# Second attention of a four-layer model rewritten with queries on partitions, and semaphores zeroed one phase later

## The reference, cut to what matters

```
L1:  xn = x * rsqrt(mean(x*x) + 1e-6) * norm1_w;  scale, shift = cond @ film1_w + film1_b
     h  = xn * (1 + scale) + shift
     q, k, v = h @ q_w + q_b, h @ k_w + k_b, h @ v_w + v_b
     p  = softmax(q @ k.T / 16)                   # one head, 256 queries x 256 keys
     x  = x + (p @ v) @ proj_w + proj_b
```

## Time and profile before

| | |
|---|---|
| median of 3 runs | 3744.56 us (3743.07 to 3746.08) |
| profiled execution: time, span | 3743.7 us, 3741.9 us |
| L1a, first transfer to last write of x | 1103.85 to 1404.89 us: 301.04 us |
| busy share of the span: PE, DVE, ACT, POOL | 86%, 61%, 46%, 22% |
| mean granted clock of PE | 0.929 |

### The profile page before, as it was taken

One profiled execution on the slowest core, in us unless ns is written; L12 is line 12 of the kernel. 1 busy time (PEld: TensorE's weight loads), 2 busy tenths in 40 slices (PEclk: granted clock), 3 DMA queues, 4 the chain that ended last, 5 costly groups with the idle time before them and its releaser, 6 DMA issues. The chain is left out here.

```text
span 3741.9 us, 71958 instructions
## 1 busy us (share of the span) xinstructions
PE 3219.6 (86%) x26636; PEld 2628.5 (70%) x26636; DVE 2298.1 (61%) x4257; ACT 1712.5 (46%) x3102; POOL 809.2 (22%) x644
## 2 busy tenths in 40 slices
PE   5899999997988877979999699699999999971686
PEld 3677777775977767967777588477777776761576
DVE  3556665655656655657777566566656656637664
ACT  1344444443543324545455354466666666610353
POOL 1211111111111101112232211312212222130453
PEclk8999999998999888989999799799999999965798
DMA  4000000001010000010000000100000000030243
GB/s 146 10 6 6 6 3 6 6 6 32 23 31 0 0 0 24 0 64 0 0 0 0 30 17 23 49 1 0 0 0 0 0 0 0 0 115 2 77 117 66
DMA packets 64848, 80.79 MB, mean 22 GB/s; under 512 B 9730, under 2 KB 56706, under 8 KB 64500
## 3 DMA queue, kind: packets, MB, share of 16 engines
q1 hardware_dynamic: 58628, 71.27, 6.4%
q0 software_dynamic: 6144, 8.52, 1.2%
HBM read 66.93 MB, written 12.85 MB: 21 GB/s over the span
## 5 line engine op out<-in xcount | busy, mean ns | idle before, releaser
L1385 POOL TENSOR_TENSOR L0a_prob<-L0a_prob 128x1024 f32<-128x1024 f32 x48 | 117.1, 2439 | 570.9 <-PE L0a_o L1743 570.9
L1487 ACT ACTIVATE L0a_prob<-L0a_st 128x512 f32<-128x512 f32 x256 | 138.7, 596 | 201.1 <-PE L0a_st L1710 174.4
L1391 POOL TENSOR_TENSOR L3a_shift<-L3a_neg,L3a_mx 128x256 fp32r<-128x256 f32 x128 | 95.8, 749 | 555.9 <-DVE L3a_mx L1968 553.9
L1487 ACT ACTIVATE L3a_prob<-L3a_st 128x512 f32<-128x512 f32 x256 | 138.7, 596 | 128.5 <-PE L3a_st L1710 128.5
L1968 DVE TENSOR_REDUCE L0a_mx<-L0a_s 128x2 f32<-128x512 f32 x256 | 164.4, 684 | 39.3 <-PE L0a_s L1686 37.5
L2286 ACT ACTIVATE L2a_prob<-L2a_st 128x512 f32<-128x512 f32 x256 | 132.2, 603 | 117.6 <-PE L2a_st L2326 117.6
L1958 DVE SCALAR_TENSOR_TENSOR L3a_qk_lo<-L3a_raw,cols_sb,L3a_qk_hi 128x256 fp32r<-128x256 f32 x256 | 156.5, 651 | 36.6 <-ACT L3a_qk_hi L1478 36.6
L1968 DVE TENSOR_REDUCE L3a_mx<-L3a_s 128x2 f32<-128x512 f32 x256 | 163.8, 680 | 18.1 <-PE L3a_s L1686 18.1
L2563 DVE TENSOR_REDUCE L2a_mx<-L2a_s 128x2 fp32r<-128x512 f32 x256 | 163.5, 681 | 15.2 <-PE L2a_s L2326 15.2
L1907 DVE RECIPROCAL L0a_rsum<-L0a_sum 128x256 f32<-128x256 f32 x16 | 28.1, 1758 | 197.7 <-PE L0a_sum L1758 176.1
L1907 DVE RECIPROCAL L3a_rsum<-L3a_sum 128x256 f32<-128x256 f32 x16 | 28.1, 1758 | 174.4 <-PE L3a_sum L1758 155.3
(11 more groups left out here) (633 smaller groups left out, 11846.6 us busy)
## 6 DMA issues: line engine op xcount, KB each, us to landing
moe_stage<-in_moe_w SPq DMA_DIRECT2D x16, 1024.0 KB, 9.0
x_sb<-in_x SPq DMA_DIRECT2D x1, 4096.0 KB, 24.6
L0a_gate<-gate_rows SPq DMA_DIRECT2D x32, 128.0 KB, 3.8
L0m_gate<-gate_rows SPq DMA_DIRECT2D x32, 128.0 KB, 3.8
L2a_gates<-gate_rows SPq DMA_DIRECT2D x2, 2048.0 KB, 12.5
L2m_gate<-gate_rows SPq DMA_DIRECT2D x32, 128.0 KB, 3.8
out_x<-x_sb SPq DMA_DIRECT2D x1, 4096.0 KB, 14.2
token_rows<-x_sb SPq DMA_DIRECT2D x1, 4096.0 KB, 27.7
```

The source lines that it names most:

```text
L1385: nc.gpsimd.tensor_tensor(both[:, :, :, 0:N], both[:, :, :, 0:N], both[:, :, :, N:2 * N], ALU.add).then_inc(halves_done, 1)
L1391: nc.gpsimd.tensor_tensor(shift[:, u % 4, :, :, :], neg64[:].unsqueeze(1).unsqueeze(1).to_broadcast([P, 2, TT, 64]), mx[:, u % 2, :, :].un ...
L1487: A(prob[:, u % 4, h, :], st_ps[u % 2][h][:], ACT.Exp, scale=64 ** -0.5).then_inc(p_done, 1)
```

## The change

`attention` is removed, and `head256` written for the one-head case takes its place in `L1a`. The scores are made once, with queries on partitions and in three passes. DVE finds each row's maximum and scales it (`maxima`), ACT takes the exponential with that as its bias and gives the row's sum as a second output (`accum_out`), PE turns the exponentials with four 128x128 transposes (`turn_probs`), and ACT copies them to SBUF. The value product has no rows of sums. Instead the reciprocal of the two sums for each partition scales the projected output, in the instruction that adds it to x (`residual`). The bias of v is added from a row. POOL now normalises the tokens (line 398) besides adding the bias row. A pass of the loop holds the attention of batch i, q, k and v of batch i+1, the transposes and the modulation of i+2, the moments of i+3 and the projection of i-1. All four weight matrices have a buffer each and are loaded at once. SP zeroes, inside each phase and behind the transfers that it issues, the semaphores of the phase before; the block of POOL is gone. The last phase's are zeroed by SP in a block of their own.

```diff
-        yield sem
-        with nc.Block() as block:
-            @block.gpsimd
-            def _(pool):
-                for s in made:
-                    pool.sem_clear(s)
+    yield sem
+    g["used_ctx"].close()
+    g["used"], g["used_ctx"] = made, ctx
+
+def clear_used(engine, g):
+    for s in g["used"]:
+        engine.sem_clear(s)
...
-                  ("L1a", lambda: attention(nc, t, g, Attention("L1a", 1, 256, 256 ** -0.5, False, "rms", 1e-6))),
+                  ("L1a", lambda: head256(nc, t, g, "L1a")),
...
+        @block.sync                                  # head256
+            for n, name in enumerate(names):
+                sp.dma_start(raw[:, n, :]..., t[f"{nm}_{name}"]...).then_inc(w_in[n], 16)
+            sp.dma_start(y_row[:], t["L1_cond_proj_b"].partition_broadcast(P)).then_inc(rows_in, 16)
+            sp.wait_ge(rows_in, 16)
+            clear_used(sp, g)
+        @block.gpsimd
+            def tokens(j, first):
+                gated_wait(ve_done, j + 1)
+                nc.gpsimd.tensor_tensor(rstd[:], ve[:], g["mhalf"][:, 0:TT], ALU.pow).then_inc(rstd_done, 1)
+                if not first:
+                    gated_wait(tp_done, j)
+                nc.gpsimd.tensor_tensor(xn[:], tiles, rstd[:]..., ALU.mult).then_inc(xn_done, 1)
+                nc.gpsimd.tensor_tensor(tiles, tiles, y_row[:]..., ALU.add).then_inc(x_biased, 1)
+        @block.scalar
+            def x_hi(j, first):
+                act.wait_ge(xm_done, j + 1)
+                act.wait_ge(v_done, j)
+            def exponentials(j):
+                for qt in range(TT):
+                    act.wait_ge(nmx_done, TT * j + qt + 1)
+                    A(prob[:, qt, :], s_ps[qt][:, 0:N], ACT.Exp, bias=nmx[:, qt:qt + 1], scale=scale,
+                      accum_out=total[:, qt:qt + 1]).then_inc(p_done, 1)
+            def body(i, more, more2):
+                exponentials(i)
+                qk_hi(i + 1, 0)
+                act.wait_ge(pt_done, i + 1)
+                A(prob_t[:]..., pt_ps[:], ACT.Copy).then_inc(pt_taken, 1)
+                qk_hi(i + 1, 1)
+                x_hi(i + 2, False)
+                act.wait_ge(pv_done, i + 1)
+                A(o[0][:]..., o_ps[:], ACT.Copy).then_inc(ohi_done, 1)
+        @block.tensor
+            def scores(j, first):
+                pe.wait_ge(qklo_done, KD * j + KD)
+                pe.wait_ge(p_done, TT * j)
+                for qt in range(TT):
+                    for c in range(KD):
+                        last = three(s_ps[qt][:, 0:N], [x[:, c, qt * P:(qt + 1) * P] for x in q],
+                                     [x[:, c, :] for x in k_], c == 0, c == KD - 1)
+                    last.then_inc(s_done, 1)
+            def body(i, n, more, more2):
+                scores(i, n == 0)
+                queries_keys(i + 1, 0, False)
+                project(i - 1, n == 1, i + 2 if more else B)
+                turn_probs(i, n == 0)
+                queries_keys(i + 1, 1, False)
+                transposes(i + 2, n + 2)
+                values(i + 1, False)
+                weighted(i, n == 0)
+        @block.vector
+            def maxima(j):
+                for qt in range(TT):
+                    dve.wait_ge(s_done, TT * j + qt + 1)
+                    V.tensor_reduce(mx[:, qt:qt + 1], s_ps[qt][:, 0:N], AX.X, ALU.max).then_inc(mx_done, 1)
+                    dve.wait_ge(mx_done, TT * j + qt + 1)
+                    V.tensor_scalar(nmx[:, qt:qt + 1], mx[:, qt:qt + 1], -scale, None, ALU.mult).then_inc(nmx_done, 1)
+            def residual(j):
+                for tt in range(TT):
+                    V.scalar_tensor_tensor(x, y_ps[:, tt * D:(tt + 1) * D], share[:, tt:tt + 1], x, ALU.mult, ALU.add)
+            def body(i, first, more, more2, more3):
+                maxima(i)
+                take_values(i, first)
+                qk_low(i + 1, 0)
+                residual(i - 1)
+                shares(i, first)
+                moments(i + 3, False)
+                qk_low(i + 1, 1)
+                modulate(i + 2, False)
+                x_low(i + 2)
+                o_low(i)
```

More of the change, by code:

```diff
@@ L701, in _ @@
-            x_hi(0)
-            loader(act=act)[1]()
-            if masked:
-                act.wait_ge(kb_done, 1)
-            body(0, True, False)
-            with act.Fori(1, B - 1) as i:
-                body(i, False, False)
-            body(B - 1, False, True)
-            tail_rows(B - 1)
-            for n in range(a.pieces):
-                over(B - 1, n)
+            A = nc.scalar.activation
+            def x_hi(j, first):
+                act.wait_ge(xm_done, j + 1)
+                if not first:
+                    act.wait_ge(v_done, j)
+                A(xt[0][:], xm[:], ACT.Copy).then_inc(xhi_done, 1)
@@ L713, in _ @@
+            x_hi(0, True)
+            for n in range(4):
+                act.wait_ge(w_in[n], 16)
+                A(w_hi[:, n, :], raw[:, n, :], ACT.Copy).then_inc(whi_done, 1)
+            qk_hi(0, 0)
+            qk_hi(0, 1)
+            x_hi(1, False)
+            with act.Fori(0, B - 2) as i:
+                body(i, True, True)
+            body(B - 2, True, False)
+            body(B - 1, False, False)
         @block.tensor
@@ new lines, in weighted @@
+            def weighted(j, first):
+                pe.wait_ge(v_taken, j + 1)
+                pe.wait_ge(pt_taken, j + 1)
+                if not first:
+                    pe.wait_ge(olo_done, j)
+                for c in range(KD):
+                    for kt in range(TT):
+                        last = mm(o_ps[:, c * N:(c + 1) * N], v[:, kt, c * P:(c + 1) * P], prob_t[:, kt, :],
+                                  start=(kt == 0), stop=(kt == TT - 1))
+                last.then_inc(pv_done, 1)
@@ L943, in _ @@
+            body(B - 1, 2, False, False)
+            project(B - 1, False, B)
         @block.vector
@@ new lines, in _ @@
+            moments(0, True)
+            for c in range(KD):
+                b = COL_AT["L1_cond_v_b"] + c
+                V.tensor_scalar(v_diag[:, c, :], g["ident"][:], cols[:, b:b + 1], None, ALU.mult).then_inc(diag_done, 1)
+            modulate(0, True)
+            x_low(0)
+            for n in range(4):
+                dve.wait_ge(whi_done, n + 1)
+                V.tensor_tensor(w_lo[:, n, :], raw[:, n, :], w_hi[:, n, :].bitcast(F32), ALU.subtract).then_inc(wlo_done, 1)
+                if n == 1:
+                    moments(1, False)
@@ new lines, in _ @@
+            qk_low(0, 0)
+            qk_low(0, 1)
+            modulate(1, False)
+            moments(2, False)
+            x_low(1)
+            dve.wait_ge(spread_done, 1)
+            V.tensor_copy(v_row[:], pt_ps[:, 0:D]).then_inc(v_row_done, 1)
+            dve.wait_ge(v_row_done, 1)
+            body(0, True, True, True, True)
+            with dve.Fori(1, B - 3) as i:
+                body(i, False, True, True, True)
+            body(B - 3, False, True, True, False)
+            body(B - 2, False, True, False, False)
@@ L1227, in heads64 @@
+            body(B - 1, False, False, False, False)
+            residual(B - 1)
 def heads64(nc, t, g, nm):
@@ L3477, in program, with _ @@
         experts(nc, t, g, out, moe)
+        with nc.Block() as block:
+            @block.sync
+            def _(sp):
+                clear_used(sp, g)
+        g["used_ctx"].close()
 def _laid_out(np, inputs):
```

928 lines of the change are left out of this document (196 added, 732 removed).

## The result

The changed kernel takes 3591.8 us (median of 4 runs, 3588.6 to 3594.4) against 3743.8 us for the kernel before beside it. The ratio is 0.9596, with a 95% interval from 0.958 to 0.9613, so it is 4.0% faster. I had forecast 3612. The profiled execution took 3589.24 us with a span of 3587.4, which is 154.5 us less than the one before.

What follows compares the result with a forecast made beforehand. L1a was taken as bound by PE plus a chain over ACT and DVE that PE cannot cover. From 3743.7 us, 105.6 for L1a and 26 for the zeroing came off, giving 3612 us; range 3592 to 3646.

Steps and rivals of the forecast that it cites:

- rival 4: L1a loop: POOL and `x_low` miss each other, the loop runs at PE's 10.6 us; 3598 to 3604 us; 10%.
- Which engine closes last: New L1a loop: DVE's queue, with ACT's steps between that DVE waits on, closes last; 11.2 us a batch.
- a batch, 11.2 for 10.74: L1a loop: 10.1 us of DVE's queue with handing over, 1.0 for POOL, 0.1 for the exponential's second output: 11.2 us.
- The ends: Start and end of L1a beyond its batches: the phase as 16 x 11.2 plus 16.2 us, 195.4 in all.
- POOL beside DVE: L1a loop: POOL's operations hold up DVE's `x_low`; taken as 1.0 us a batch, between nothing and 2.6.
- Rival 1: L1a loop: both POOL operations hold DVE in each batch, 12.7 us a batch; +21, 3633 us; 15%.
- PE's lower bound: L1a loop: PE's own work for a batch at 2.4 GHz, 10.6 us, as the lower bound of a batch.
- rival 2: L1a loop: clock stays at 0.88, 12.1 us a batch, 3625 us, 8%; at 1.2 GHz throughout 3721 us, 2%.
- Zeroing: Nine phase boundaries: 364 zeroings moved to SP are covered, 24.8 us, plus 1.3 for blocks; 26 us.
- rival 3: Phase boundaries: zeroing stays on the path because SP ends last in its phases; 24.8 us come back, 3637 us; 4%.
- that a boundary costs only its gap: Phase boundaries: the 26 us gain counted only zeroings and blocks, nothing for the phases behind.
- Slower or serial: L1a: batches don't overlap, 20.6 us each, kernel 3763 us; decided from a batch of 19.4 us; 1%.

Runs made afterwards that it cites:

- bias_behind: Changed kernel, with POOL's addition of the bias row waiting until DVE has made the low part of the tokens: 3578.2 us.
- value_at_once: Changed kernel, with PE's value product right behind the turning of the exponentials, ahead of the second half of the next q and k: 3614.8 us.
- same_again: The changed kernel once more, unedited, as a yardstick for runs on the same chip: 3594.3 us.

## Why the prediction was right, point by point

**The number: inside the range, and partly by luck.** Three terms missed in the same direction, by 9.6 us in L1a, 3.1 in the gaps and 4 to 9 in the other phases, as told below. I had set the low end of 3592 by rival 4, in which POOL and `x_low` miss each other, and they met in each batch of the loop. The range held the result to within the scatter, but not for the reason that I gave for its low end.

**Which engine closes last: right, and shown.** DVE's queue, with ACT's steps in it, was the circuit. The filler on PE was free, and taking 1.04 us out of DVE's queue shortened the batch by 1.03. Between the starts in the timeline after, the circuit reads: maxima to second exponential 1.19 (I had 1.16), the exponential 0.46 (0.49), q and k on ACT 0.87 (0.9), `qk_low` 0.79 (0.88), `residual` 0.97 (0.88), `share` 0.24 (0.16), `moments` 1.41 (1.45), `qk_low` 0.80 (0.88), `modulate` up to ACT 1.09 (1.00), `x_hi` 0.67 (0.62), `x_low` 1.65 (1.69), `o_low` 0.60 (0.69), which is 10.74.

**Term mis-sized: a batch, 11.2 for 10.74.** I added whole recorded durations and then 0.4 for handing over. In DVE's row of instructions the next one starts some 0.1 us before the record of the last one ends (1186.79 against 1185.14 + 1.73 = 1186.87), so the recorded durations already covered the handing over. That is 16 x 0.46 = 7.4 of the 9.6 us by which L1a came out shorter than my 195.4. The ends, 185.83 - 16 x 10.74 = 14.0, against 16.2, are the other 2.2.

**POOL beside DVE: right.** I took 1.0; it was 1.03 to 1.07 in 13 batches. The trace agrees with the rule of the Trainium skill that I cited (page "SBUF — State Buffer", section "Who interferes with whom"): POOL's operation was issued 0.11 us earlier and kept its 1.29 us, and the DVE operation ended 0.55 us after it, at 1186.87 against 1186.32. Rival 1, held by both operations, didn't occur, because the first of them was over (1184.84) before `x_low` began.

**PE's lower bound: 10.6 was too high.** It is 9.71 (bias_behind, PE busy throughout). The value product takes 1.54 us up to the next start (I had 1.82), and the first of a row behind single-pass products costs nothing extra (1188.37 to 1188.49, 0.12 like any other). So rival 4 was mis-sized; with PE as the bound the time is 3578, not 3598 to 3604.

**The clock: rival 2 fell.** The granted clock is 1.00 with PE busy 92% of the loop, and also 1.00 in value_at_once with 87% (83.04 of 95.20), where before it was 0.88 at 83%. What decides it in the old loop stays open.

**Zeroing: right in kind, 26 for 29.1 in the gaps.** A block cost 0.27 instead of 0.15, and (29.1 - 9 x 0.27) / 364 = 0.073 us each zeroing, instead of 0.068. The gaps around L1a are 0.28 us each, where I had expected about 1. No phase of the changed kernel shows SP ending last: every gap ahead of a phase from L0m on is 0.28 to 0.5 us, so rival 3 didn't occur.

**The step that failed: that a boundary costs only its gap.** I counted nothing for the phases behind. In the profiled pair they took 10.2 us less; about 2.5 of that is luck of the profiled execution, and by the timed pairs it is 4 to 9. It comes with a lower clock at the start of three phases (L0m, L2a, r); that the clock is the whole cause was not tested. With 9.6 from L1a, 3.1 from the gaps and 10.2 from here, the 22.9 us between 3612.1 and the profiled 3589.2 are accounted for.

**Slower or serial: no.** One batch overlaps the next, and the order on PE that does it is worth 2.2 us a batch (value_at_once against bias_behind); even without it the batch is at 11.9, far from the 19.4 at which it would decide.

## What to carry to other kernels

Price a loop by the distances between starts, engine by engine, and ask of the slowest queue which of its operations have two inputs in SBUF and what POOL does at that time: one wait on POOL that moved an addition back by 1 us was worth 14 us here, and the version with it, at 3578.2 us (ratio to the kernel before 0.956, interval 0.9547 to 0.9573), is faster than the kernel before and, by 0.4%, than the changed one (its runs take 3577.3 to 3584.1, those of same_again on the same chip 3591.1 to 3597.6). A filler that is free shows that PE is not the bound, and the same filler paid in full that it has become it. Work at phase boundaries on which all engines wait costs its own length and here some 4 to 9 us more in the phases behind, so put it on an engine that has nothing to do inside the next phase.

## What the runs showed of the hardware that was not expected

- An exponential with a sum as its second output leaves a further row of 0.19 us (`ACTIVATION_READ_ACCUMULATOR`), and the next ACT instruction starts 0.1 us before that row ends. The exponential itself takes 0.47 us against 0.385 for the plain one in the earlier trace rows; that goes with its bias, which is a column now and a constant before, since an operation of ACT of the same size with a bias column and no sum takes 0.468 in the earlier trace rows. From start to start the exponential costs 0.46 (1188.58 to 1189.04) and the operation without a sum behind it 0.36 (1189.04 to 1189.40).
- The loop of the changed kernel loads ACT's table in every batch (1.28 us), although all its functions alternated without a load in the loop before. One exponential ahead of the loop removed the loads.
- A normalising operation of POOL over 128x512 (line 398) took 1.04 us, where its addition over the same size takes 1.27 to 1.30. The first reads one value of `rstd` for each tile as its second operand, the second a whole row; whether that is the reason was not tested.
